# Local attention normalised behind the values' product, and new slots for softplus, copies, heads and tail, in a hybrid block kernel

## The chip, the cores and the metric

The kernel runs on one core of one Trainium2 chip. The metric is the device time in microseconds (us) of the whole kernel, 8 sequences (batches) in one launch. Engines are named as in the profile: PE (TensorE), DVE (VectorE), ACT (ScalarE), POOL (GpSimd) and SP (SyncE, which only issues DMAs here).

## The reference

For each of 8 sequences of 512 tokens of width 128, after a layer norm, the block adds four branches to its input, then a second layer norm and a small linear layer with a residual:

```python
xn = (x - mu) * rsqrt(var + 1e-05) * ln_g + ln_b
delta = softplus(dt_in @ w_dt + b_dt);  A = -exp(A_log)         # 128 channels, 64 states
h = exp(dt * A) * h + (dt * xt) * bt;   y = sum_n h * ct         # over 512 steps
scores = q @ k3 / sqrt(8) + bias       # 16 heads, 4 key heads, blocks of 32 queries, 96 keys
ao = softmax(mask(scores)) @ v3
conv = silu(conv4(x) + b_conv)
mem = x @ w_wm + b_wm + 0.3 * softmax(x @ dec.T / sqrt(128)) @ dec     # 512 memory rows
x1 = x + 0.2 * ao @ wo + 0.45 * (y + x * D) @ w_ssm_out + 0.15 * conv + 0.2 * mem
out = x1 + LN(x1) @ W2 + bias
```

## The kernel before

The state recurrence sets the frame. The 128 channels times 64 states are cut into 64 *units* (one unit: 2 channels by 64 states on 128 partitions, 512 steps along the free axis). Every engine has its own instruction stream, in which `body(B, p)` walks the 64 *slots* of batch B; the engines meet only at semaphores. In slot s:

- PE copies the input of unit s+2 to all state rows (`unit_u`, L911). In every fourth slot it sums a group of products over the states (`reduce_group`, L935).
- ACT takes the exponential of the decays of unit s+2 (`unit_exp`, L665). Both wait for the scan of unit s-2, whose buffers they fill again.
- DVE multiplies the unit's input by B (`unit_input`, L1189, three units of four) and runs the scan of unit s-1 (`unit_scan`, L1201).
- POOL multiplies two scanned units by C in odd slots (`pair_product`, L1389), and does the input product of each fourth unit (`pool_input`, L1405).

All else is hung into these slots by tables of numbers at the top of the file. `SCORES_AT` starts one of 16 attention blocks in slots 6, 9, ..., 51, and the `_LAG` numbers say how many slots later each of its steps stands: bias and maximum on DVE (2), exponentials on ACT (3 and 4), the reciprocal of the sums on DVE (6), the division of the probabilities on POOL (`prob_norm`, L1394, listed at 5), the transposes on PE (`prob_transposes`, L951, 9), their copy on ACT (9), the product with the values on PE (`values`, L959, 11), and its copy on ACT (`ao_copy`, L695, 11). All four blocks of transposes and the values' result share one PSUM bank, `ptP`, so that the transposes of block k wait for `ao_copy` of block k-1.

`JOB_AT` places the matrix jobs that share the bank `jobP` (families p: next batch's projections; m: memory attention and convolution; t: the tail of the batch before). `AT` places the remaining steps: while batch B is scanned, its slots hold the end of batch B-1 (`project`, `residual`, `root2`, `normalise2`, `ffn`, `output`) and the preparation of batch B+1 (layer norm, softplus, the three bf16 parts of u, and q, k, v, B, C). The softplus is exp(-|x|) on ACT (L613), 1+e and back (L615, L617, for the part lost in rounding), the logarithm (L622), four steps on POOL (L332), then the parts. `normalise2` (L553) waits on POOL's `root2`. `PRE` lists the jobs that `front` runs for batch 0 before its slots, and `tail` finishes batch 7 behind its last slot.

An instruction that waits holds all that is behind it on its engine.

Of the kernel before, what the change touches and what calls it, by code (L numbers as in the profile page):

```python
# [39 lines left out]
MEM = {n: i for i, n in enumerate(["es0", "pt0", "conv", "es1", "es2", "pt1", "es3", "pt2", "pt3"])}  # L40
# [5 lines left out]
JOB_AT = {13: ("t", "back"), 15: ("p", "xaT"), 17: ("p", "xnT"), 19: ("p", "dtpre"), 21: ("p", "v"),  # L46
# [3 lines left out]
EMPTY_LAG = 0  # L50
LAST_PROJECT = {60: (0, 1), 61: (2, 3), 62: (4, 5), 63: (6, 7)}
# [4 lines left out]
    "reduce": 3, "y_copy": 5, "project": 1, "proj_copy": 12, "residual": 14, "aggr2": 16, "root2": 17,  # L56
    "normalise2": 20, "ffn": 25, "output": 29,

    "ln_stats": 0, "ln_aggr": 2, "ln_root": 4, "ln_apply": 11, "scale_xn": 12, "softplus_exp": 20,
    "softplus_logs": 21, "lost": 22, "log1p": 23, "dt": 24, "u": 25, "high": 28, "r": 30,  # L60
    "mid": 33, "lo": 35,

    "tanh": 40, "gate": 42,
# [4 lines left out]
ROWS_AT = {"store": 15, "rows": 14}  # L68
VALUE_DMA_AT = {4: (0, 1, 2, 3, 4, 5), 5: (6, 7, 8), 6: (9, 10, 11)}
PART_DMA_AT = {16: 0, 18: 1, 20: 2}  # L70
# [6 lines left out]
BIAS_LAG, EXP_LAG, INV_LAG, NORM_LAG, PT_LAG, PT_COPY_LAG, PV_LAG, AO_COPY_LAG = 2, (3, 4), 6, 5, 9, 9, 11, 11  # L77
# [38 lines left out]
def hybrid_block_kernel(nc, x, ln_g, ln_b, w_xproj, w_dt, b_dt, A_log, D_ssm, w_ssm_out, wq, wk, wv,  # L116
# [3 lines left out]
    with ctx:  # L120
# [138 lines left out]
        p_exp, p_inv, p_norm = sem("p_exp"), sem("p_inv"), sem("p_norm")  # L259
# [92 lines left out]
        def _(sp):  # L352
# [23 lines left out]
            def store_rows(B, p):  # L376

                wait(sp, sp_step, B * N_SP + SP["u"])
                sp.dma_start(dt_rows[p], dtv[:, :]).then_inc(rows_out, 16)
                sp.dma_start(u_rows[p], uv[32 * POOL_Q:32 * POOL_Q + 32, :]).then_inc(urows_out, 16)  # L380
# [23 lines left out]
            def body(B, p):  # L404
                for m in range(UNIT_PAIRS):
# [13 lines left out]
                    if not last(B):  # L419
                        if m == ROWS_AT["rows"]:  # L420
                            store_rows(B + 1, 1 - p)
# [53 lines left out]
            def front(B, p):  # L475
                load_weights()
                bias_out()
                store_rows(B, p)
                spread_parts(sp, B, p, 0)
                widen(B, p, 0)  # L480
                bias_back()
# [988 lines left out]
```

## Time and profile before

| | |
|---|---|
| median of 3 runs | 1112.58 us (1109.39 to 1113.99) |
| the profiled execution | 1114.23 us, of it 1112.4 us span |
| busy DVE, POOL | 979.3 us (88%), 955.6 us (86%) |
| busy ACT, PE | 837.5 us (75%), 830.9 us (75%) |
| slot 0 of batches 0 to 6 on DVE (layer norm statistics) | 37.3, 176.6, 308.8, 439.4, 571.5, 704.5, 834.6 us |
| last scan, last instruction on DVE | ends near 1086 us, 1109.7 us |

The span has a front of 37 us, eight batches of 130 to 139 us, and a tail of 23 us. Busy shares are means over stages in which different waits end last; the views of one stage tell more than they do. In a view of one engine's instructions, a bracket shows how long the engine sat idle before the instruction and what released it. In a view of waits the columns are the total, the number and the longest.

### The profile page before, as it was taken

Reading aid. Unit: us, or ns where it says so; the run is one execution under the profiler, and the core shown is the slowest. Engines: PE = TensorE matmul, PEld = TensorE weight load, DVE = VectorE, ACT = ScalarE, POOL = GpSimd, SP = SyncE. Lnnn points to the kernel's source line nnn. Section 1 sums busy time; section 2 is a strip of 40 time slices with the busy share of each in tenths; the row PEclk is TensorE's granted clock in tenths of the full one; section 3 lists DMA queues with packets and bytes.
Section 4 is the critical chain, followed back from the end, with each engine's and each line's share of the span. In section 5 each row is a group of like instructions: output and inputs, shape, how many; then the busy total and the mean of one; then the engine's idle time right before and its main releaser. Section 6 shows DMA issues by size and latency. Waiting matters only on the chain. (4 is left out here: it accounts for less than half of the span.)

```text
span 1112.4 us, 19145 instructions
## 1 busy us (share of the span) xinstructions
PE 830.9 (75%) x4151; PEld 339.3 (30%) x4151; DVE 979.3 (88%) x2299; ACT 837.5 (75%) x2255; POOL 955.6 (86%) x675
## 2 busy tenths in 40 slices
PE   5367878688777786877778777867868778677775
PEld 2023333233323332333323333323332333232332
DVE  2688999979997999979999699897999799999991
ACT  4468886788778878687877887679887887858871
POOL 6369988989898988988899898899989898979892
PEclk9556998978997989979898798888899798989897
DMA  5845667647675666666676476665666566766630
GB/s 111 196 126 169 180 159 185 171 138 198 163 183 155 185 167 159 172 157 172 168 203 161 128 191 162 167 173 159 177 176 183 153 187 165 188 161 164 196 95 9
DMA packets 124391, 181.18 MB, mean 163 GB/s; under 512 B 29263, under 2 KB 41056, under 8 KB 124256
## 3 DMA queue, kind: packets, MB, share of 16 engines
q1 hardware_dynamic: 123968, 179.56, 61.4%
q14 instruction: 96, 0.79, 0.3%
q8 instruction: 39, 0.64, 0.3%
q10 hardware_dynamic: 288, 0.20, 0.1%
HBM read 170.79 MB, written 5.05 MB: 158 GB/s over the span
## 5 line engine op out<-in xcount | busy, mean ns | idle before, releaser
L1389 POOL TENSOR_TENSOR prod<-hst,C 128x1024 f32<-128x1024 f32 x256 | 602.0, 2354 | 94.9 <-DVE hst L1201 94.4
L1201 DVE TENSOR_TENSOR_SCAN hst<-decay,bank 128x512 f32<-128x512 f32 x384 | 459.5, 1209 | 3.0 <-DVE cv_a L1236 2.8
L1189 DVE TENSOR_TENSOR bank<-bank,B 128x512 f32<-128x512 f32 x384 | 263.1, 685 | 52.6 <-PE bank L911 34.8
L665 ACT ACTIVATE decay<-wide,A_rep 128x512 f32<-128x512 f32 x384 | 273.4, 715 | 41.5 <-DVE hst L1201 31.2
L911 PE MATMUL bank<-spread,sel_bc 96*128 96x512 bf16 x384 | 164.5, 434 | 101.0 <-DVE hst L1201 90.6
L679 ACT ACTIVATE prob<-s_sb,nmax 128x96 f32<-128x96 f32 x512 | 185.2, 365 | 0.9 <-DVE nmax L1214 0.5
L1405 POOL TENSOR_TENSOR uwide<-uwide,B 128x512 f32<-128x512 f32 x128 | 162.7, 1271 | 22.5 <-DMA uwide<-u_rows 22.5
L935 PE MATMUL bank<-prod,sel_red 128*32 128x512 f32 x1024 | 164.9, 722 | 0.0
L1201 DVE TENSOR_TENSOR_SCAN hst<-bank,uwide 128x512 f32<-128x512 f32 x128 | 155.4, 1214 | 2.7 <-POOL uwide L1405 2.7
L951 PE MATMUL bank<-ident,prob 128*96 128x128 f32 x512 | 85.9, 295 | 77.5 <-ACT ao L695 58.3
L944 PE MATMUL bank<-k,q 128*128 128x384 f32 x256 | 126.7, 580 | 22.3 <-DVE nmax L1214 22.2
L688 ACT ACTIVATE probT<-bank 96x512 f32<-96x512 f32 x128 | 74.9, 585 | 72.0 <-PE bank L951 71.6
L911 PEld LDWEIGHTS bank<-spread,sel_bc 96*128 96x128 bf16 x384 | 40.2, 106 | 228.0 <-DVE hst L1201 176.5
L665 ACT ACTIVATE bank<-wide,A_rep 128x512 f32<-128x512 f32 x128 | 87.2, 681 | 26.8 <-DVE hst L1201 26.6
L1394 POOL TENSOR_TENSOR prob<-prob,pinv 128x384 f32<-128x384 f32 x128 | 105.8, 826 | 0.0
L951 PEld LDWEIGHTS bank<-ident,prob 128*96 128x96 f32 x512 | 61.3, 137 | 135.4 <-issue 102.6
L1214 DVE CUSTOM_DVE_ANT_0 s_sb<-bank,bias 128x96 f32<-128x96 f32 x512 | 98.3, 250 | 0.0
L679 ACT ACTIVATION_READ_ACCUMULATOR prob<-s_sb,nmax 128x1 f32 x512 | 98.1, 192 | 0.0
L944 PEld LDWEIGHTS bank<-k,q 128*128 128x128 f32 x256 | 48.9, 216 | 87.0 <-DVE nmax L1214 48.6
L959 PE MATMUL bank<-probT,vw 96*8 96x128 f32 x1024 | 57.0, 298 | 14.7 <-ACT probT L688 9.8
L695 ACT ACTIVATE ao<-bank 128x128 f32<-128x128 f32 x128 | 34.1, 266 | 30.8 <-PE bank L959 30.5
L959 PEld LDWEIGHTS bank<-probT,vw 96*8 96x8 f32 x1024 | 19.9, 94 | 89.5 <-issue 57.1
(189 smaller groups left out, 1027.4 us busy)
## 6 DMA issues: line engine op xcount, KB each, us to landing
wide<-dt_rows SPq DMA_DIRECT2D x512, 256.0 KB, 4.7
uwide<-u_rows SPq DMA_DIRECT2D x128, 256.0 KB, 4.1
spread<-parts SPq DMA_DIRECT2D x66, 32.0 KB, 4.1
x_sb<-in_L_attn_x_dram SPq DMA_DIRECT2D x8, 256.0 KB, 4.5
dt_rows<-sp_t SPq DMA_DIRECT2D x8, 256.0 KB, 2.6
out_dram<-outb SPq DMA_DIRECT2D x8, 256.0 KB, 3.9
vw<-v_tok SPq DMA_DIRECT2D x80, 16.0 KB, 3.3
u_rows<-uv SPq DMA_DIRECT2D x8, 64.0 KB, 2.4
```

What stands on the lines that cost most here:

```text
L665: nc.scalar.activation(to, wide[m % SLOTS][:, s % 2, :], ACT.Exp, scale=A_rep[:, g:g + 1]).then_inc(exp_done, 1)
L679: ins = nc.scalar.activation(prob[:, k % 4, g, :], s_sb[:, k % 2, g, :], ACT.Exp, bias=nmax[:, k % 2, g:g + 1], scale=-1.0, accum_out=psum ...
L911: mm(uP[q][:, :], sel_bc[:, i, :, :].rearrange("k j n -> k (j n)"), spread[p][:, q, :], start=True, stop=True).then_inc(u_ready, 1)
L935: ins = mm(yP[32 * q:32 * q + 32, :], sel_red[:, i, :], prod[:, (i % 2) * 4 + q, :], start=(i == 0), stop=(i == GROUPS - 1), skip_group_ch ...
L944: mm(sP[:, 0:KVH * 3 * W], q4[:, k, :, :].rearrange("p r q -> p (r q)"), k4[:, :, k * W:k * W + 3 * W], start=True, stop=True).then_inc(s_ ...
L951: ins = nc.tensor.transpose(ptP[0:3 * W, g * 128:(g + 1) * 128], prob[:, k % 4, g, :], ident[:, :])
L1189: v.tensor_tensor(uP[s % 4][:, :], uP[s % 4][:, :], B2[p][:, :], ALU.mult).then_inc(dbx_done, 1)
L1201: v.tensor_tensor_scan(hst[:, s % 8, :], kept, into[:, :], 0.0, ALU.mult, ALU.add).then_inc(scan_done, 1)
L1214: ins = v.tensor_tensor_reduce(s_sb[:, k % 2, g, :], sP[:, g * 3 * W:(g + 1) * 3 * W], bias3[:, row, g, :], 1.0, BIG, ALU.add, ALU.min, nm ...
L1389: g.tensor_tensor(prod[:, 2 * (m % 4):2 * (m % 4) + 2, :], hst[:, 2 * (m % 4):2 * (m % 4) + 2, :], C2[p][:, :].unsqueeze(1).to_broadcast([ ...
L1394: g.tensor_tensor(prob[:, k % 4, :, :], prob[:, k % 4, :, :], pinv[:, k % 4, :].unsqueeze(2).to_broadcast([128, KVH, 3 * W]), ALU.mult) \
L1405: g.tensor_tensor(u, u, B2[p][:, :], ALU.mult).then_inc(gbx_done, 1)
```

## The change

1. **Attention.** The probabilities stay undivided. PE transposes them directly behind the exponentials (lag 6, was 9), multiplies by the values (lag 8, was 11), and in four further small products spreads the reciprocal sums over 32 rows each, into columns 128 to 255 of the same bank. ACT copies 256 columns of the bank (was 128; lag 9, now at the head of the slot behind `unit_exp`), and POOL multiplies the two halves (`output_norm`, 128 elements a partition; before, 384).
2. **Softplus and second norm.** The three ACT steps that stood in slot 20 stand in slots 24, 25 and 26; the logarithm moves from 21 to 28; `normalise2` from 20 to 23, `root2` from 17 to 19. The jobs B and C move from 34 and 35 to 24 and 25. POOL's four steps stand at 29 to 32 and not 22 to 25, the parts at 35 to 41. SP's stores and loads of these move with them.
3. **Heads.** `project` starts in slot 2 (was 1); the jobs `pt2`, `pt3` and `q` come one to two slots earlier.
4. **Front.** For batch 0 ACT goes from exp to the logarithm directly, DVE does 1+e and back in one instruction; dt is stored before u is there; two unit exponentials go ahead of the copies of q, and the copies of k go into slot 1.
5. **Tail.** Batch 7's projections start at slot 58 (was 60); terms 6 and 7 go ahead of the last reduction, 8 and 9 behind it; the bias of the last linear layer goes into the scores' bank, ahead of the second norm's transposes.

```diff
-MEM = {n: i for i, n in enumerate(["es0", "pt0", "conv", "es1", "es2", "pt1", "es3", "pt2", "pt3"])}
+MEM = {n: i for i, n in enumerate(["es0", "conv", "es1", "pt0", "es2", "pt1", "es3", "pt2", "pt3"])}
...
-          23: ("t", "zT"), 26: ("t", "ffn"), 30: ("m", "es0"), 34: ("p", "B"), 35: ("p", "C"), 37: ("m", "pt0"),
+          24: ("p", "B"), 25: ("p", "C"), 26: ("t", "zT"), 29: ("t", "ffn"), 33: ("m", "es0"),
...
-LAST_PROJECT = {60: (0, 1), 61: (2, 3), 62: (4, 5), 63: (6, 7)}
+LAST_PROJECT = {58: (0,), 59: (1,), 60: (2, 3), 61: (4, 5)}
...
-    "normalise2": 20, "ffn": 25, "output": 29,
+    "normalise2": 23, "ffn": 28, "output": 31,
...
-BIAS_LAG, EXP_LAG, INV_LAG, NORM_LAG, PT_LAG, PT_COPY_LAG, PV_LAG, AO_COPY_LAG = 2, (3, 4), 6, 5, 9, 9, 11, 11
+BIAS_LAG, EXP_LAG, INV_LAG, NORM_LAG, PT_LAG, PT_COPY_LAG, PV_LAG, AO_COPY_LAG = 2, (3, 4), 6, 9, 6, 6, 8, 9
...
-        prob = sb("prob", [128, 4, KVH, 3 * W])
+        prob = sb("prob", [128, 2, KVH, 3 * W])
...
+        ao_raw = sb("ao_raw", [128, 2, 2, 128])
...
                 nc.scalar.activation(sp_e[:, :], sp_e[:, :], ACT.Exp, scale=-1.0).then_inc(sp_step, 1)
+
+            def softplus_sum(B):
                 wait(act, sp_step, B * N_SP + SP["exp"])
                 nc.scalar.activation(sp_t[:, :], sp_e[:, :], ACT.Identity, bias=1.0).then_inc(sp_step, 1)
+
+            def softplus_less(B):
                 wait(act, sp_step, B * N_SP + SP["sum"])
                 nc.scalar.activation(sp_t[:, :], sp_t[:, :], ACT.Copy, bias=-1.0).then_inc(sp_step, 1)
 
             def softplus_logs(B):
 
-                wait(act, sp_step, B * N_SP + SP["less"])
+                wait(act, sp_step, B * N_SP + SP["exp" if first(B) else "less"])
...
-                    wait(act, pt_ready, B * NBLK + k - 3)
+                    wait(act, pt_ready, B * NBLK + k - 1)
...
                 wait(act, pv_ready, B * NBLK + k + 1)
-                if k == 0:
-                    wait(act, ready["t"], B * N_TAIL - N_TAIL + 1)
-                nc.scalar.activation(ao4[:, :, k * W:(k + 1) * W],
-                                     ptP[:, 0:128].rearrange("p (r q) -> p r q", r=REP), ACT.Copy).then_inc(ao_evac, 1)
+                wait(act, ao_norm, B * NBLK + k - 1)
+                nc.scalar.activation(ao_raw[:, k % 2, :, :].rearrange("p a c -> p (a c)"), ptP[:, 0:256],
+                                     ACT.Copy).then_inc(ao_evac, 1)
...
-                wait(pe, p_norm, B * NBLK + k + 1)
+                wait(pe, p_exp, B * NBLK + k + 1)
...
-                    ins = mm(ptP[32 * g:32 * g + HD, 0:128], vw[:, k, g, :], probT[:, g, :], start=True, stop=True)
+                    mm(ptP[32 * g:32 * g + HD, 0:128], vw[:, k, g, :], probT[:, g, :], start=True, stop=True)
+                wait(pe, p_inv, B * NBLK + k + 1)
+                for g in range(KVH):
+                    ins = mm(ptP[32 * g:32 * g + 32, 128:256], pinv[:, k % 4, g:g + 1].to_broadcast([128, 32]), ident[:, :],
+                             start=True, stop=True)
...
-                for n in range(8, N_PROJ - 1):
-                    project(B, p, n)
+                project(B, p, 6)
+                project(B, p, 7)
                 reduce_group(B, GROUPS - 1)
+                project(B, p, 8)
+                project(B, p, 9)
                 project(B, p, N_PROJ - 1)
                 tail_job("back", B, p)
+                wait(pe, s_max, NB * NBLK)
+                ffn_bias(sP)
                 tail_job("zT", B, p)
-                ffn_begin(B)
-                tail_job("ffn", B, p)
+                wait(pe, done["t"], job_count("t", B, "zT"))
+                ffn_half(0, sP)
+                filled(ffn_half(1, sP), "t", B, "ffn")
...
+                dve.wait_ge(sp_step, SP["exp"])
+                v.tensor_scalar(sp_t[:, :], sp_e[:, :], 1.0, 1.0, ALU.add, ALU.subtract).then_inc(sp_step, 2)
...
-            def prob_norm(B, k):
-                wait(pool, p_inv, B * NBLK + k + 1)
-                g.tensor_tensor(prob[:, k % 4, :, :], prob[:, k % 4, :, :],
-                                pinv[:, k % 4, :].unsqueeze(2).to_broadcast([128, KVH, 3 * W]), ALU.mult) \
-                    .then_inc(p_norm, 1)
+            def output_norm(B, k):
+
+                wait(pool, ao_evac, B * NBLK + k + 1)
+                if k == 0:
+                    wait(pool, ready["t"], B * N_TAIL - N_TAIL + 1)
+                g.tensor_tensor(ao4[:, :, k * W:(k + 1) * W], ao_raw[:, k % 2, 0, :].rearrange("p (r q) -> p r q", r=REP),
+                                ao_raw[:, k % 2, 1, :].rearrange("p (r q) -> p r q", r=REP), ALU.mult).then_inc(ao_norm, 1)
...
```

In the order of instructions, the first place is ACT in the body, from the second norm (`outb`) to the exponential behind the logarithm. `xn`, `sp_t` and `sp_l` are the softplus's tiles, `fT` the copy of job zT. Before:

```order
L553 ACTIVATE outb<-x,nbz,rz 128x128 x3
L695 ACTIVATE ao<-bank 128x4x32 [waits pv_ready]
L613 ACTIVATE xn<-xn 128x512 [waits sp_step]
...
L615 ACTIVATE sp_t<-xn 128x512 [waits sp_step]
...
L617 ACTIVATE sp_t<-sp_t 128x512 [waits sp_step]
...
L665 ACTIVATE bank<-wide,A_rep 128x512 [waits scan_done]
...
L688 ACTIVATE probT<-bank 96x512 [waits pv_ready,pt_ready]
...
L622 ACT_TABLE_LOAD
L622 ACTIVATE sp_l<-xn 128x512 [waits sp_step]
...
L665 ACT_TABLE_LOAD
```

and now:

```order
L560 ACTIVATE outb<-x,nbz,rz 128x128 x3
...
L705 ACTIVATE ao_raw<-bank 128x256 [waits ao_norm,pv_ready]
...
L599 ACTIVATE B_0<-bank 128x512 [waits p_job_ready]
L620 ACTIVATE xn<-xn 128x512 [waits sp_step]
...
L599 ACTIVATE C_0<-bank 128x512 [waits p_job_ready]
...
L624 ACTIVATE sp_t<-xn 128x512 [waits sp_step]
...
L748 ACTIVATE fT<-bank 128x512 [waits t_job_ready]
...
L628 ACTIVATE sp_t<-sp_t 128x512 [waits sp_step]
...
L633 ACT_TABLE_LOAD
L633 ACTIVATE sp_l<-xn 128x512 [waits sp_step]
...
L676 ACT_TABLE_LOAD
```

What stood within two slots now stands in six, with the copies of B, C and zT between.

The second place is PE within one attention block (`prob` the probabilities, `vw` the values, `pinv` the reciprocal sums, `sel_bc` the unit's input). Before:

```order
L951 MATMUL bank<-ident,prob 96x128 [waits ao_evac,p_norm]
L951 MATMUL bank<-ident,prob 96x128 x3
...
L911 MATMUL bank<-spread,sel_bc 128x512 [waits scan_done]
L959 MATMUL bank<-probT,vw 8x128 [waits pt_evac]
L959 MATMUL bank<-probT,vw 8x128 x3
```

and now:

```order
L967 MATMUL bank<-ident,prob 96x128 [waits ao_evac,p_exp]
L967 MATMUL bank<-ident,prob 96x128 x3
...
L927 MATMUL bank<-spread,sel_bc 128x512 [waits scan_done]
L975 MATMUL bank<-probT,vw 8x128 [waits pt_evac]
L975 MATMUL bank<-probT,vw 8x128 x3
L978 MATMUL bank<-ident,pinv 32x128 [waits p_inv]
L978 MATMUL bank<-ident,pinv 32x128 x3
```

The transposes no longer wait for POOL, and four products on `pinv` follow the values.

The third place is PE behind the last slot (`dec_m`, `wo_p`, `w_ssm`: terms of the projection). Before:

```order
L935 MATMUL bank<-prod,sel_red 32x512 x3
L1000 MATMUL bank<-ao,wo_p 128x512 [waits ao_evac] x4
L935 MATMUL bank<-prod,sel_red 32x512 [waits prod_done]
L935 MATMUL bank<-prod,sel_red 32x512 x3
L1003 MATMUL bank<-yT,w_ssm 128x512 [waits y_evac]
...
L820 MATMUL bank<-ident,outb 128x128 [waits l2_step,t_job_done]
L820 MATMUL bank<-ident,outb 128x128 x3
L1015 MATMUL bank<-bias_row,ones_row 128x512 [waits t_job_done]
L1008 MATMUL bank<-W,fT 128x128 x4
```

and now:

```order
L1020 MATMUL bank<-ao,wo_p 128x512 [waits ao_norm] x2
L951 MATMUL bank<-prod,sel_red 32x512 [waits prod_done]
L951 MATMUL bank<-prod,sel_red 32x512 x3
L1020 MATMUL bank<-ao,wo_p 128x512 [waits ao_norm] x2
L1023 MATMUL bank<-yT,w_ssm 128x512 [waits y_evac]
...
L1039 MATMUL bank<-bias_row,ones_row 128x512 [waits s_max]
L836 MATMUL bank<-ident,outb 128x128 [waits l2_step,t_job_done]
L836 MATMUL bank<-ident,outb 128x128 x3
L1028 MATMUL bank<-W,fT 128x128 [waits t_job_done]
L1028 MATMUL bank<-W,fT 128x128 x3
```

Two of the four `wo_p` terms stand behind the last reduction, and the bias product ahead of the second norm's transposes.

## Rows read from the trace of the kernel before

**Rows 1.** The page: busy time, share of the span and instructions of each engine.

```profile
PE 830.9 (75%) x4151; PEld 339.3 (30%) x4151; DVE 979.3 (88%) x2299; ACT 837.5 (75%) x2255; POOL 955.6 (86%) x675
```

**Rows 2.** The waits, longest first: who waited for whom, total us, times, longest.

```profile
PE bank L951 <- ACT ao L695: 58.3, 38, 3.9
...
DVE bank L1189 <- PE bank L911: 34.8, 24, 8.1
...
DVE pinv L1222 <- ACT prob L679: 25.3, 8, 3.8
...
DVE bank L1189 <- PE bank L944: 14.3, 14, 2.4
...
PE bank L990 <- ACT k L572: 7.6, 5, 1.7
```

**Rows 3.** DVE in order of time, batch 4, slots 23 to 33: the idle times.

```profile
619.24 0.70 DVE L1189 TENSOR_TENSOR bank<-bank,B 128x512 f32<-128x512 f32 x1 [2.31 <-PE bank L911]
...
624.77 0.18 DVE L1222 RECIPROCAL pinv<-psum_r 128x4 f32<-128x4 f32 x1 [3.71 <-ACT prob L679]
...
634.44 0.70 DVE L1189 TENSOR_TENSOR bank<-bank,B 128x512 f32<-128x512 f32 x1 [2.44 <-PE bank L944]
```

**Rows 4.** ACT in order of time, the same place of batch 4.

```profile
614.42 1.65 ACT L553 ACTIVATE outb<-x,nbz,rz 128x128 f32<-128x128 f32 x4 [0.62 <-POOL nbz L1411]
615.98 0.25 ACT L695 ACTIVATE ao<-bank 128x128 f32<-128x128 f32 x1
616.13 0.62 ACT L613 ACTIVATE xn<-xn 128x512 f32<-128x512 f32 x1
...
620.06 1.28 ACT L622 ACT_TABLE_LOAD   x1
621.36 0.63 ACT L622 ACTIVATE sp_l<-xn 128x512 f32<-128x512 f32 x1
622.00 1.28 ACT L665 ACT_TABLE_LOAD   x1
623.30 0.72 ACT L665 ACTIVATE decay<-wide,A_rep 128x512 f32<-128x512 f32 x1
```

**Rows 5.** PE in order of time, the same place of batch 4, and once behind it.

```profile
616.37 0.85 PE L951 MATMUL bank<-ident,prob 128*96 128x128 f32 x4 [3.38 <-ACT ao L695]
...
619.56 1.94 PE L935 MATMUL bank<-prod,sel_red 128*32 128x512 f32 x8
...
639.97 1.06 PE L935 MATMUL bank<-prod,sel_red 128*32 128x512 f32 x8
```

**Rows 6.** Busy us by stretch: that place in batch 4, and the same slots of batch 7.

```profile
616.00:640.00 24.00, 20.60 (x98) 9.67 (x99) 15.31 (x43) 20.43 (x57) 20.05 (x15) 0.72 0.44 129
1002.00:1020.00 18.00, 13.76 (x87) 5.73 (x79) 17.02 (x44) 13.67 (x44) 17.77 (x16) 0.90 0.71 181
```

The columns are: stretch, length, busy PE, PEld, DVE, ACT, POOL with instruction counts, granted clock, DMA share, GB/s.

**Rows 7.** The stretch of batch 7 for the scans (L1201) alone: busy DVE and count.

```profile
1002.00:1020.00 18.00, 10.91 (x10) 0.90 0.71 181
```

**Rows 8.** The page: groups of instructions, busy us, mean ns, idle before.

```profile
L1394 POOL TENSOR_TENSOR prob<-prob,pinv 128x384 f32<-128x384 f32 x128 | 105.8, 826 | 0.0
...
L959 PE MATMUL bank<-probT,vw 96*8 96x128 f32 x1024 | 57.0, 298 | 14.7 <-ACT probT L688 9.8
```

**Rows 9.** PE in order of time behind the last slots of batch 7.

```profile
1089.15 3.70 PE L1000 MATMUL bank<-ao,wo_p 128*128 128x512 f32 x8
1092.78 1.06 PE L935 MATMUL bank<-prod,sel_red 128*32 128x512 f32 x8
1094.57 1.13 PE L1003 MATMUL bank<-yT,w_ssm 128*128 128x512 f32 x2 [0.72 <-ACT yT L671]
...
1104.88 2.07 PE L1015 MATMUL bank<-bias_row,ones_row 1*128 1x512 f32 x2 [0.69 <-ACT fT L738]
```

**Rows 10.** POOL and PE in order of time: the last products, and the first inputs.

```profile
1082.02 6.97 POOL L1389 TENSOR_TENSOR prod<-hst,C 128x1024 f32<-128x1024 f32 x3
...
36.01 1.44 PE L911 MATMUL bank<-spread,sel_bc 96*128 96x512 bf16 x3 [9.44 <-DMA spread<-parts]
```

More of the change, by code:

```diff
@@ L648, in front @@
                             spread_parts(act, B, p, part)
+                        for s in range(AHEAD):
+                            unit_exp(B, s)
                         act.wait_ge(const_ready, 3)
                         act.wait_ge(head_tables, 3)
-                    if name == "k":
-                        for s in range(AHEAD):
-                            unit_exp(B, s)
-                    pre_job(name, B, p, front=True)
+                    if name != "k":
+                        pre_job(name, B, p, front=True)
             def unit_exp(B, s):
@@ L757, in body @@
                         unit_exp(B + 1, s + AHEAD - UNITS)
+                    k = block_at(s, AO_COPY_LAG)
+                    if k is not None:
+                        ao_copy(B, k)
                     if first(B):
+                        if s == 1:
+                            pre_job("k", B, p, front=True)
                         setup_step(s - SETUP_AT)
@@ L773, in body @@
                         probT_copy(B, k)
-                    k = block_at(s, AO_COPY_LAG)
-                    if k is not None:
-                        ao_copy(B, k)
                     t = memory_tile_at(s, M_EXP_LAG)
@@ L796, in body @@
                             softplus_exp(B + 1)
+                        if s == AT["sum"]:
+                            softplus_sum(B + 1)
+                        if s == AT["less"]:
+                            softplus_less(B + 1)
                         if s == AT["softplus_logs"]:
@@ L998, in project @@
                 elif n < 10:
-                    wait(pe, ao_evac, (B + 1) * NBLK)
+                    wait(pe, ao_norm, (B + 1) * NBLK)
                     ins = mm(jobP[:, :], wo_p[:, n - 6, :], ao4[:, n - 6, :], start=False, stop=False)
@@ L1004, in project, with ffn_half @@
                     filled(ins, "t", B, "proj")
-            def ffn_half(h):
+            def ffn_half(h, job=jobP):
                 for t in (2 * h, 2 * h + 1):
-                    ins = mm(jobP[:, t * D:(t + 1) * D], zT[:, t * 128:(t + 1) * 128], W2[:, :], start=False, stop=True,
+                    ins = mm(job[:, t * D:(t + 1) * D], zT[:, t * 128:(t + 1) * 128], W2[:, :], start=False, stop=True,
                              skip_group_check=True)
@@ L1014, in ffn_begin, with ffn_bias @@
                 fill("t", B, "ffn")
-                mm(jobP[:, :], ones_row[:, :], bias_row[:, :].unsqueeze(1).to_broadcast([1, NT, D]), start=True, stop=False,
+                ffn_bias(jobP)
+                ffn_half(0)
+            def ffn_bias(job):
+                mm(job[:, :], ones_row[:, :], bias_row[:, :].unsqueeze(1).to_broadcast([1, NT, D]), start=True, stop=False,
                    skip_group_check=True)
-                ffn_half(0)
             def tail_job(name, B, p):
@@ L1220, in inverse_sums @@
                 wait(dve, p_exp, B * NBLK + k + 1)
-                wait(dve, p_norm, B * NBLK + k - 3)
+                wait(dve, pv_ready, B * NBLK + k - 3)
                 v.reciprocal(pinv[:, k % 4, :], psum_r[:, k % 4, :]).then_inc(p_inv, 1)
@@ L1423, in body @@
                     if k is not None:
-                        prob_norm(B, k)
+                        output_norm(B, k)
                     if not first(B):
```

38 lines of the change are left out of this document (21 added, 17 removed), and 4 rows, old and new, of the table JOB_AT.

## The prediction, made before the changed kernel was run

> **What bounds the kernel now.** I read the page first. DVE is busy 979.3 us of 1112.4 and POOL 955.6 [rows 1], so DVE cannot end much before about 1037: its work plus some 58 us of front and tail (the first scan input comes at 36 us, the last scan ends 23 us before DVE's last instruction). The rest of DVE's idle time is 1112.4 - 979.3 - 58 = 75 us, and only that can be won in the batches. Then I read the waits: DVE waits for PE's unit inputs 34.8 us (8.1 of it once, in the front), for ACT's probabilities 25.3 us in 8 waits, for PE's scores 14.3 us [rows 2]. It hardly ever waits for POOL, so taking work from POOL is worth nothing by itself. Third, DVE in order of time. Each of batches 1 to 6 has the same hole in slots 23 to 31: 2.31 + 3.71 + 2.44 = 8.5 us in batch 4 [rows 3]. The others are 8.5, 6.9, 8.5, 6.1 and 6.9 us, together 45.5 or 7.6 a batch; batch 0 has 4.3, batch 7 has 1.0.
>
> Fourth, what the releasers did. ACT works without a pause through the second norm, three softplus steps, the logarithm and two table loads of 1.28 us [rows 4]. `ao_copy` stands behind the norm, PE's transposes wait 3.38 us for it, and the next unit input is queued behind them on PE [rows 5]; the exponentials of the scores stand behind the table loads, and DVE's reciprocal waits 3.71 us for them [rows 3]. The third gap is an echo: after PE's pause its granted clock in that stretch is 0.72, against 0.90 in batch 7 [rows 6], a mix of its two levels, 1.2 and 2.4 GHz; a reduction takes 1.94 us at the lower one where it takes 1.06 later [rows 5]. Batch 7 prepares no further batch, so it has no softplus, and there the hole is all but gone. That is the best evidence: the burst on ACT makes the hole.
>
> **Softplus, norm and copies (the largest term).** In batch 7 10 scans take 18.0 us [rows 7], so a slot is 1.8 us; ACT is busy 13.67 us of these [rows 6], so it has 24% or 0.43 us a slot to spare. Before, slots 19 to 23 hold on top: two 512-column steps of 0.6 us (job dtpre), the norm with its wait on POOL (0.62 + 1.6), three softplus steps (3 x 0.65), v (0.26), the logarithm with its loads (1.28 x 2 + 0.65 = 3.2), zT (0.6) [rows 4], together 9.4 us. Five slots spare 2.2, so ACT falls 7.2 us behind, and the first two gaps are 6.0: some 1.2 us are covered by the two slots that ACT and PE run ahead.
> After, the same sort of work stands in slots 21 to 28: 1.2 + 1.6 + 0.26 + 3 x 0.65 + 3.2 + zT 0.6, and now B and C too (2 x 0.6), 10.0 us; eight slots spare 3.4, so the backlog peaks at 6.6 us behind slot 28. The norm's wait on POOL (0.62) goes, since it stands 4 slots behind `root2` and not 3. With 1.2 us of cover that leaves 5.4 us; `output` at slot 31 gives ACT another 0.8 us of DVE time, so 4.6. The unevenness speaks for less: the scores' exponentials of slot 28 now stand ahead of the loads, the 3.7 us wait thus has no cause of its own, and with shorter pauses the echo (1.6 us on average) should not come. I take 4.0 us a batch in place of 7.6: -3.6 x 6 = -21.5 us, and -2 in batch 0 (half of its 4.3). Bounds: the hole as it is (0), and as in batch 7 (6 x 6.6 + 3.3 = -43).
> The trace has no drain in a table load: the logarithm starts 0.02 us behind a load that takes 1.28 [rows 4]. The Trainium skill ("ScalarE: Activation LUTs", What ACT_TABLE_LOAD costs) adds a drain of about 1.38 us to each switch, 2.66 us in all. By it the group in slot 28 would be 5.9 us long and not 3.2, and the sum would be 6 x 2.7 = 16 us higher; the row decides, and I leave it out.
>
> **Attention, POOL.** It loses 105.8 us of `prob_norm` [rows 8] and gets 128 products of a third of the size. By size that is 0.28 us each (826/3), bounded by 0.2 and 0.83: 36 us, bounds 25 and 106. So POOL falls by about 70 us, and by the waits above this buys nothing directly. The wait of the norm on `root2` gets shorter, which is in the term above. The new wait, POOL's `output_norm` on ACT's copy, holds `pair_product` and `pool_input` behind it. POOL starts slot s only when the scan of unit s is there, two slots behind ACT, so it costs nothing as long as ACT is less than 3.6 us late.
>
> **Attention, PE.** Four products of 128 columns a block are added, in four column groups, as `values` has. That row is busy 57.0 us in 128 blocks, 0.45 us a block for eight passes [rows 8]; mean 298 ns each shows that they overlap. I take 0.45, bounds 0.25 (a quarter of a reduction's 1.06, rows 5) and 2.4 (8 x 298 one behind the other). That is +57 us of PE work, 7 us a batch on 830.9; bounds 32 and 307. PE waits 58.3 us for `ao_copy` [rows 2] and more for scans, so this lies in pauses, except in slots 2 to 12, where `project` fills PE (see heads).
> The transposes wait no longer for DVE and POOL. They wait for `ao_copy` of the same slot, where before it was the slot before; ACT has it first behind `unit_exp`. That takes about 1 us of the lead of the unit inputs, and costs only where ACT is late already: +0, bounds 0 and +12 (1 us in each of 12 blocks).
>
> **Attention, ACT and DVE.** The copy has 256 columns for 128. From 0.25 us for 128 columns and 0.62 for 512 it will take 0.35 to 0.4 us [rows 4], 128 x 0.1 = 13 us more, of ACT's 275 idle. DVE's part does not change.
>
> **Heads.** PE waits 7.6 us in five waits for the copies of k before `project` [rows 2], and behind these DVE has gaps, 14 us over seven batches in slots 1 to 12. `project` one slot later takes that wait away, and the earlier `pt` and q jobs thin out ACT there. Against it stands the new PE work: 3 or 4 blocks in those slots, 1.6 us a batch. I take -2 us, bounds -12 and +12. The gaps at other places (some 0.8 us a batch around slot 52) get +2 us, since the jobs there move closer to the products.
>
> **Front.** Two ACT steps like the softplus step of 0.62 us in [rows 4], 0.65 with their gap, go from the chain exp, logarithm, parts, spread, first unit input [rows 10]; DVE's single instruction lies beside the table load. dt is stored one DVE step (0.7 us) earlier. -2 us, bounds -3 and +1 (u is stored later, and unit 3 needs it).
>
> **Tail.** POOL ends its last product at 1088.99, but PE reduces it only at 1092.78, since four `wo_p` terms stand ahead [rows 9, 10]. After, the reduction starts at 1089, ends at 1090.1, two terms (1.85) cover the copy of y, and the last term starts at 1091.95 and not 1094.57: -2.6. PE is free in time, for its earlier terms start two slots sooner. The bias product of 2.07 us stands on the chain [rows 9] and goes under the second norm: -2.1. Together -4.7, bounds -2 and -6.
>
> **Sum.** -21.5 - 2 + 0 - 2 + 2 - 2 - 4.7 = -30 us. From the profiled execution's 1114.2 that gives 1084; it lies 1.6 us above the median of the runs, so I forecast 1083 against 1112.6, or 2.7% faster.
>
> **Rivals.**
> *The hole closes* (0.24). If the lateness of ACT is covered by slots 24 to 28, only batch 7's 1.0 us remains: -43, heads -8, front and tail -6.7: 1055. For it: the three causes of rows 3 are each moved away from one another. Against it: 10.0 us of ACT work in eight slots do not fit into 3.4, and B and C now stand in the middle of it.
> *The hole moves* (0.12). It is as long as before in slots 24 to 33, since the logarithm with its loads is undivided and the transposes wait on the same slot's copy. Then the front, the tail and the heads remain, -8.7: 1104 against the median. For it speaks that backlogs of 7.2 and 6.6 us hardly differ.
> *PE becomes the bound* (0.06). Where PE's work in a slot passes 1.8 us, each added product delays the next unit input. In batch 7 it is busy 13.76 of 18.0 us at a clock of 0.90 [rows 6], so it has 0.42 us a slot, and a block's 0.45 us falls on three slots. At the clock of the hole it would not fit: 20.60 of 24.0 are taken [rows 6]. If the clock stays low, all 57 us come on the path, against gains of 30: 1140. It decides when PE has less than 0.15 us a slot left.
>
> What POOL does is no rival, for if its relief brought nothing at all the sum would be the same.
>
> **Numbers.** The forecast has 0.58 (its own range 1070 to 1095). The range for 8 in 10 goes from 1060, most of the way to the first rival and short of all bounds together, to 1104, the second. Half a per cent is 5.6 us, about what a measurement of this kernel can tell from no change: the second rival is half inside it. Faster 0.86, same 0.07, slower 0.07.
>
> **What would show it.** Batches 1 to 6 should take about 126 us each (now 130 to 133). DVE's gaps in slots 23 to 33 should sum to 3 to 5 us a batch, behind the logarithm at slot 28 to 31 and not before it; the wait of the reciprocal for the probabilities should fall from 25.3 to under 8 us. POOL's busy time should be near 885 us, PE's near 885, ACT's near 850. The new products should be busy about 57 us. On the end, the bias product should stand beside the second norm, and DVE's last instruction 18 us behind the last scan. The forecast is wrong if the waits for unit inputs stay above 30 us, or if new waits of DVE for PE are spread over all blocks.

## The result, and the profile after

| | after | before |
|---|---|---|
| median | 1187.53 us (1183.06 to 1189.20, 4 runs) | 1112.65 us |
| ratio, 95% interval | 1.0671 [1.0634, 1.0709] | |
| profiled execution, its span, its granted clock | 1187.11 us, 1185.3 us, 0.857 | 1114.23 us, 1112.4 us, 0.871 |

The changed kernel is 6.7% slower, where 2.7% faster was forecast: 104 us lie between the forecast and the measurement. The experiments below find them in two lines of the change, and with these two mended the kernel runs at 1083.2 us. Of all the runs reported here, one of experiment 8 (2344 us) and three of the kernel before in the last set were in a slower state and are left out of medians and ratios.

The page's busy times, which answer to [rows 1]:

```profile
PE 866.9 (73%) x5175; PEld 368.5 (31%) x5175; DVE 987.3 (83%) x2300; ACT 854.8 (72%) x2253; POOL 910.3 (77%) x675
```

No engine's work explains the loss: DVE has 8 us more, PE 36, POOL 45 less. The idle time of DVE grew by 65 us. The waits (total us, times, longest), which answer to [rows 2]:

```profile
PE bank L967 <- ACT ao_raw L705: 86.4, 68, 4.7
DVE x L1273 <- PE bank L836: 59.9, 8, 9.0
PE bank L975 <- DMA vw<-v_tok: 44.2, 7, 7.2
DVE bank L1219 <- PE bank L927: 38.7, 32, 8.0
DVE pinv L1252 <- ACT prob L690: 16.9, 8, 3.1
DVE bank L1219 <- PE bank L960: 14.6, 15, 3.1
```

Two rows are new in size. The transposes of the probabilities wait 86.4 us for ACT's copy (58.3 before), and PE waits 44.2 us for transfers of `vw`, the values, seven times: once in each of batches 1 to 7. DVE's wait for the residual (`x`, L1273) is its echo. Batch 1 in order of time, first SP's queue, then PE, then DVE:

```profile
197.49 3.89 SPq L462 DMA_DIRECT2D vw<-v_tok  x6
201.54 1.27 SPq L407 DMA_DIRECT2D wide<-dt_rows  x2
202.91 2.25 SPq L462 DMA_DIRECT2D vw<-v_tok  x3
205.29 1.50 SPq L407 DMA_DIRECT2D wide<-dt_rows  x2
206.89 1.93 SPq L462 DMA_DIRECT2D vw<-v_tok  x3
```

```profile
210.94 0.61 PE L975 MATMUL bank<-probT,vw 96*8 96x128 f32 x8 [6.38 <-DMA vw<-v_tok]
211.33 0.65 PE L978 MATMUL bank<-ident,pinv 128*32 128x128 f32 x8
211.91 0.61 PE L927 MATMUL bank<-spread,sel_bc 96*128 96x512 bf16 x1
212.45 1.94 PE L951 MATMUL bank<-prod,sel_red 128*32 128x512 f32 x8
214.32 1.65 PE L960 MATMUL bank<-k,q 128*128 128x384 f32 x2
```

```profile
217.59 0.69 DVE L1273 TENSOR_TENSOR x<-bank,x_sb 128x512 f32<-128x512 f32 x1 [8.17 <-PE bank L836]
...
243.09 0.18 DVE L1252 RECIPROCAL pinv<-psum_r 128x4 f32<-128x4 f32 x1 [3.14 <-ACT prob L690]
```

SP issues 12 transfers of values one after another, 0.64 to 0.75 us each, starting only when block 0 has its scores; the last issue ends at 208.8. The values' product of block 0 now stands in slot 14 instead of 17, so it waits 6.38 us, and the next input, the reduction and the scores stand behind it, at the lower clock as well (1.94 us where [rows 5] also has 1.06). DVE then idles 8.17 us. Its gaps at this place in batches 1 to 7 are 8.17, 6.37, 6.76, 6.80, 9.04, 6.33 and 8.44, together 51.9 us.

The hole that the prediction followed got shorter and now stands in slots 28 and 29, but it shrank less than forecast: its two large gaps are 3.14 + 1.49 us in batch 1 and together 3.9 to 5.5 in batches 2 to 6, and all gaps of slots 23 to 33 come to 5.4 us a batch, where 4.0 was taken. The tail and the products:

```profile
1172.10 0.69 DVE L1273 TENSOR_TENSOR x<-bank,x_sb 128x512 f32<-128x512 f32 x1 [7.94 <-PE bank L836]
...
1181.86 0.69 DVE L1291 TENSOR_TENSOR outb<-bank,x 128x512 f32<-128x512 f32 x1 [7.64 <-PE bank L1028]
```

```profile
L975 PE MATMUL bank<-probT,vw 96*8 96x128 f32 x1024 | 54.9, 289 | 49.1 <-DMA vw<-v_tok 44.2
L1427 POOL TENSOR_TENSOR ao<-ao_raw 128x128 f32<-128x128 f32 x128 | 58.4, 456 | 15.3 <-ACT ao_raw L705 15.1
```

From the start of the last scan to that of `outb` it is 18.9 us (23.75 before). The values' row [rows 8] kept its busy time, but its idle time rose from 14.7 to 49.1.

### The profile page after: what moved, and what is told of

Same layout as the page of the kernel before. It is cut to its first block and busy times, and to the rows that moved or that the text cites. A ratio compares the mean times of both kernels' runs of the same rounds, so it can differ in the third digit from the quotient of the medians.

```text
span 1185.3 us, 21303 instructions
## 1 busy us (share of the span) xinstructions
PE 866.9 (73%) x5175; PEld 368.5 (31%) x5175; DVE 987.3 (83%) x2300; ACT 854.8 (72%) x2253; POOL 910.3 (77%) x675
## 5 line engine op out<-in xcount | busy, mean ns | idle before, releaser
L1219 DVE TENSOR_TENSOR bank<-bank,B 128x512 f32<-128x512 f32 x384 | 263.0, 685 | 64.5 <-PE bank L927 38.7
L951 PE MATMUL bank<-prod,sel_red 128*32 128x512 f32 x1024 | 173.5, 757 | 0.3 <-POOL prod L1419 0.3
L967 PE MATMUL bank<-ident,prob 128*96 128x128 f32 x512 | 90.5, 307 | 86.4 <-ACT ao_raw L705 86.4
L960 PE MATMUL bank<-k,q 128*128 128x384 f32 x256 | 123.6, 567 | 6.6 <-DVE nmax L1244 6.2
L975 PE MATMUL bank<-probT,vw 96*8 96x128 f32 x1024 | 54.9, 289 | 49.1 <-DMA vw<-v_tok 44.2
L705 ACT ACTIVATE ao_raw<-bank 128x256 f32<-128x256 f32 x128 | 47.2, 369 | 35.0 <-PE bank L978 34.8
L1427 POOL TENSOR_TENSOR ao<-ao_raw 128x128 f32<-128x128 f32 x128 | 58.4, 456 | 15.3 <-ACT ao_raw L705 15.1
L960 PEld LDWEIGHTS bank<-k,q 128*128 128x128 f32 x256 | 46.2, 206 | 71.2 <-issue 52.5
L1001 PE MATMUL bank<-mdiag,mprob 128*128 128x128 f32 x256 | 45.0, 331 | 17.2 <-ACTq L717 9.2
```

The lines of the kernel that those rows point to most:

```text
L951: ins = mm(yP[32 * q:32 * q + 32, :], sel_red[:, i, :], prod[:, (i % 2) * 4 + q, :], start=(i == 0), stop=(i == GROUPS - 1), skip_group_ch ...
L960: mm(sP[:, 0:KVH * 3 * W], q4[:, k, :, :].rearrange("p r q -> p (r q)"), k4[:, :, k * W:k * W + 3 * W], start=True, stop=True).then_inc(s_ ...
L967: ins = nc.tensor.transpose(ptP[0:3 * W, g * 128:(g + 1) * 128], prob[:, k % 2, g, :], ident[:, :])
L1219: v.tensor_tensor(uP[s % 4][:, :], uP[s % 4][:, :], B2[p][:, :], ALU.mult).then_inc(dbx_done, 1)
```

## The experiments

A measurement gives the median, the ratio to the kernel before and its 95% interval. The kernel before ran on the same chip each time (1117.3, 1116.6, 1115.2, 1114.2 and 1116.7 us in the five sets); the ratio is estimated from all the runs, so it is not exactly the quotient of the medians. Where an edit of numbers says enough, only that is shown.

**1. The transfers of the values earlier.**

```diff
-VALUE_DMA_AT = {4: (0, 1, 2, 3, 4, 5), 5: (6, 7, 8), 6: (9, 10, 11)}
+VALUE_DMA_AT = {0: (0, 1, 2, 3, 4, 5), 1: (6, 7, 8), 2: (9, 10, 11)}
...
-                    wait(sp, s_ready, B * NBLK + 1)
+                if not first(B):
+                    wait(sp, pv_ready, B * NBLK)
```

> The changed kernel with one edit: the twelve DMAs that lay out the values of each batch are issued at SP's steps 0 to 2 (slots 0 to 5) and not 4 to 6, and wait for the last product with the values of the batch before and not for this batch's first scores. Theory A (the first product with the values, now in slot 14 and not 17, waits for these DMAs, and PE holds all behind it): PE's wait for vw (44 us) and DVE's wait for the residual (52 us in the batches) go, 1187 falls to about 1135. Rival B (PE's added products and the transposes' wait on the same slot's copy make the kernel slower, and the DMA wait only lies where PE would wait anyway): DVE waits elsewhere for nearly the same time, 1175 or more.

Measured: 1134.94 us, 1.0166 [1.0115, 1.0217], 52.6 us less. DVE's wait for the residual is 13.4 us instead of 59.9, and PE's for the transfers is gone, as theory A said. The first cause is shown. What is left to explain is 52 us between this kernel and the forecast.

**2. The transfers late, the lags later.** The changed kernel with three buffers of probabilities and these lags:

```diff
-... = 2, (3, 4), 6, 9, 6, 6, 8, 9
+... = 2, (3, 4), 6, 12, 9, 9, 11, 12
```

> The changed kernel with the attention steps at later slots: transposes and their copy at lag 9, values at 11, copy and product at 12 (three buffers of probabilities). The values' DMAs stay where they are. Theory A: the first product with the values stands in slot 17 again, the wait for its DMAs is nearly gone, about 1135 as with the early DMAs. Rival B: all of PE's and ACT's added work and the wait on the same slot's copy are still there, 1175 or more.

Measured: 1159.01 us, 1.0346 [1.0274, 1.0418]. PE's wait for the transfers is down to 4.3 us, so the slot of the values' product decides whether their transfers are late. But the kernel was 24 us slower than experiment 1, between the two theories, and the transposes waited 98.7 us for ACT's copy, which neither theory named.

**3 and 4. The change in two parts.** First the kernel before with the attention part and the early transfers, then the changed kernel without the attention part.

> The kernel before with the attention part of the change alone (undivided probabilities, four more products, wider copy, division on POOL, new lags), with the values' DMAs early; softplus, norm, jobs, heads, front and tail as before. Theory A: PE's added 57 us lie mostly in pauses, 1113 to 1130. Rival B: 1150 or more.

> The changed kernel with the attention part taken back: the division on POOL, lags and copies as before; softplus, norm, jobs, heads, front and tail at their new places. By the sum of the prediction without the attention terms it is 1083 to 1095: DVE's hole in slots 23 to 33 falls from 7.6 to about 4 us a batch, front -2, tail -4.7. Rival C (the new places of softplus and jobs are themselves no gain, the hole only moves): 1105 or more.

Measured: 1152.17 us, 1.031 [1.0256, 1.0364], and 1109.86 us, 0.9951 [0.9918, 0.9984]. The attention part costs some 35 us beside its transfers, as rival B had it; in its trace (of the fastest of its five runs, 1140.6 us) the transposes wait 117.2 us for the copy. The rest gains little, as rival C had it: DVE's idle time in slots 21 to 34 of batches 1 to 6 falls from 7.8 us a batch to 2.8, but that in slots 35 to 47 rises from 0.5 to 4.2, where the gate waits for ACT's tanh and the memory's reciprocal for its exponentials. The change had moved the tanh and the gate two slots forward (from 40 and 42 to 38 and 40).

**5. Without the four sum products** (experiment 1's kernel; what it leaves out is the division by the right sums).

> e1 (values early) without the four products that spread the reciprocal sums; ACT still copies 256 columns, of which half are then meaningless, so the output is not divided by the right sums. Theory D (PE's added 0.45 us a block is on the path): of the 25 us that e1 lies above the rest of the change alone (1110), nearly all go, 1110 to 1118. Theory E (the order: the transposes wait for the copy of the same slot, and its copy back for them): PE's products lie in pauses, 1128 to 1135.

Measured: 1152.14 us, 1.0331 [1.0274, 1.0388]: above both theories, 17 us *slower* without products that were busy 52.8 us in experiment 1. They are thus no cost. The granted clock fell from 0.883 to 0.861, and the work that is left got longer: PE as a whole is busy 843.2 us against 844.9 with the products, the transposes of the probabilities alone 94.1 against 87.6. That led to experiment 9.

**6. The transposes a slot later** (experiment 1 with lags 7, 7 for 6, 6).

> e1 with the transposes and their copy at lag 7 and not 6, so one slot behind the copy of the block before; products and copies are all there. Theory E: 1112 to 1122, and PE's wait for the copy (86 us) falls below 60. Theory D: 1130 to 1137.

Measured: 1135.77 us, 1.0161 [1.0091, 1.0231]. The wait moved and did not shrink: PE waited 21.5 us for the copy of the values, but 97.8 for the copy of the transposed probabilities, ahead of the values. The time lies in theory D's range, but D's reason, PE's added work, is excluded by experiment 5.

**7. The gate later, without the attention part.** Slot 42 is where the kernel before has its gate.

> The rest of the change alone (e4, 1110) with the convolution one slot later (39), its gate in slot 42 and not 40 (three slots behind and not two), and the memory jobs behind it where they stood before (43 to 59, q at 60). Theory F (the gain of the softplus's new slots is lost at the gate, 2.1 us a batch, and at the memory jobs around it, and can be had): about 1095. Theory G (the hole is only ACT's work, and shows wherever DVE next needs ACT): 1105 to 1112.

Measured: 1110.45 us, 0.9935 [0.9904, 0.9966]; as experiment 4, so theory G.

**8. Front and tail alone, on the kernel before.**

> The kernel before with the changes of front and tail alone. By the prediction -6.7 us: 0.994 of before, about 1106 if before is 1112.6. If the last terms of the projection come too late in their old slots, only the bias product's 2 us and the front's 2 us show.

Measured: 1115.8 us, 0.9978 [0.9933, 1.0023]. In its trace the first scan starts 0.5 us earlier and the end behind the last scan is 2.8 us shorter; the times can't tell that from nothing.

**9. The sum products on a constant** (experiment 1; also without the right sums).

```diff
-                wait(pe, p_inv, B * NBLK + k + 1)
-                    ins = mm(..., pinv[:, k % 4, g:g + 1].to_broadcast([128, 32]), ident[:, :],
+                    ins = mm(..., ident[:, 0:32], ident[:, :],
```

> The kernel of e1 with the four sum products of a block multiplied from the constant identity instead of the reciprocals, and without the wait for the reciprocal: the output is not divided by the right sums, but the matrix engine has the same 53 us of small products as e1 and e5 has not. Theory K (the clock: with less work between its waits the matrix engine is granted less, and its chain of transposes, values and inputs gets longer; e1 0.883 and 1134.9, e5 0.861 and 1152.1): the products' work brings the time back, 1130 to 1140 at a granted clock of 0.88. Theory W (it is the order that the wait for the reciprocal makes between the vector and the matrix engine that helps e1): no wait, so the time stays with e5 at 1148 to 1156, though the clock may rise.

Measured: 1136.18 us, 1.0183 [1.0122, 1.0244], granted clock 0.875 to 0.897 in its four runs, against 0.857 to 0.861 in those of experiment 5; this is theory K. The busy times of 900 us in the middle, first of experiment 5, then of this one (stretch, length, busy PE, PEld, DVE, ACT, POOL, granted clock):

```profile
200.00:1100.00 900.00, 678.97 (x3432) 277.75 (x3430) 801.28 (x1900) 698.07 (x1867) 740.88 (x534) 0.87 0.63 164
```

```profile
200.00:1100.00 900.00, 688.77 (x4418) 298.67 (x4416) 818.48 (x1923) 708.59 (x1902) 756.17 (x543) 0.91 0.63 165
```

Nearly 1000 more matrix instructions come to only 10 us more of busy time, and DVE gets 17 us more done (the trace is of the fastest of the four runs, 1126.4 us, so some of this is its own). It is the products' work that gives the time back, not the wait on the reciprocals. That it does so through the clock fits every number here, but no run holds the clock fixed, so this step is inferred.

**10. ACT's copy of the values in the values' own slot** (experiment 1 otherwise).

```diff
-PT_COPY_LAG, PV_LAG, AO_COPY_LAG = ..., 6, 8, 9
+PT_COPY_LAG, PV_LAG, AO_COPY_LAG = ..., 6, 8, 8
...
                         unit_exp(B + 1, s + AHEAD - UNITS)
-                    k = block_at(s, AO_COPY_LAG)
-                    if k is not None:
-                        ao_copy(B, k)
...
                         probT_copy(B, k)
+                    k = block_at(s, AO_COPY_LAG)
+                    if k is not None:
+                        ao_copy(B, k)
```

> The kernel of e1 with ScalarE's copy of the values in the slot of the values themselves and behind the copy of the transposed probabilities, as the kernel before has it, instead of at the head of the next slot. Theory P (the wait of the transposes for this copy, 85.9 us in 72 waits in e1 against 58.3 in the kernel before, comes from the copy's place, and is what the attention part costs beside the values' transfers): the wait falls to 60 or less and the time to 1110 to 1122. Theory Q (ScalarE's slots are full, the wait is of its load and not of the place): wait and time stay, 1130 to 1140, or ScalarE now waits for the values ahead of its softplus or norm and the time rises above 1140.

Measured: 1083.22 us, 0.9707 [0.9639, 0.9775], better than either theory had it. The waits of experiment 1 (first) and of this one, in each the transposes for the copy and DVE for its unit inputs:

```profile
PE bank L969 <- ACT ao_raw L707: 85.9, 72, 4.7
...
DVE bank L1221 <- PE bank L929: 39.2, 32, 8.4
```

```profile
PE bank L969 <- ACT ao_raw L707: 31.1, 28, 3.5
...
DVE bank L1221 <- PE bank L929: 18.0, 19, 8.1
```

**11 and 12. The transfers early without the attention part**, on experiment 7 and on the kernel before.

> The kernel of e7 (attention as in the kernel before, the rest as in the changed one, gate and convolution a slot or two later) with the values' transfers issued in slots 0 to 2 instead of 4 to 6. The kernel before has 14.7 us of waits ahead of the values' product. Theory V (part of that wait is on the path even with the values at slot 17): 3 to 10 us less than e7, 1100 to 1107. Theory N (it is hidden, since the vector engine is two slots ahead there): 1110 as e7.

> The kernel before with the values' transfers in slots 0 to 2 and nothing else. Theory V: 3 to 10 us less than the kernel before (a ratio of 0.991 to 0.997). Theory N: within 0.3% of it. It also says how much of e3's time is of its attention part and how much of the transfers' place.

The "slots 0 to 2" of these texts are SP's steps of two slots each, as in experiment 1.

Measured: 1112.17 us, 0.9963 [0.9936, 0.9991], and 1114.03 us, 0.9983 [0.9951, 1.0014]. This is theory N twice: with the values' product at slot 17 their transfers' place is worth nothing that can be measured. It costs time only together with the new lag.

**13 and 16. The copy's place alone, both ways.** The changed kernel with only this mended, its transfers still late; and the kernel before with only this made worse (its copy moved from the end of slot 11 of a block to the head of slot 12).

> The changed kernel with ScalarE's copy of the values in the values' own slot, behind the copy of the transposed probabilities, and the values' transfers left in slots 4 to 6. Theory S (the two costs add: transfers 52 us, the copy's place 52 us): 1130 to 1140, with the residual gaps behind the transfers still there. Theory H (ScalarE's queue now stands still behind the late values as well, so that the gaps by the transfers grow): 1150 to 1175. Theory M (the copy is hidden behind the transfers): 1180 or more.

> The kernel before with ScalarE's copy of the values moved from the end of slot 11 of a block to the head of slot 12, the one edit of the attention part that e10 takes back, and nothing else. Theory P (a copy at the head of the slot of the next block's transposes makes them, and every input behind them on the matrix engine, wait for the end of ScalarE's work of that slot): the wait ahead of the transposes rises from 58 us to 85 or more and the time to 1140 to 1170. Theory Q (the place costs only together with the changed attention): 1110 to 1122.

Measured: 1139.43 us, 1.0219 [1.017, 1.0267], so 48 us less (theory S); and 1161.03 us, 1.0412 [1.0367, 1.0456], so 47 us more (theory P). The wait of the transposes fell from 86.4 us in 68 waits in the one and rose from 58.3 us in 38 waits in the other, here experiment 13 and then 16:

```profile
PE bank L967 <- ACT ao_raw L705: 33.7, 30, 3.2
```

```profile
PE bank L951 <- ACT ao L695: 131.0, 74, 6.3
```

Batch 3 of experiment 16 shows the mechanism, PE first, then ACT:

```profile
495.00 0.41 PE L959 MATMUL bank<-probT,vw 96*8 96x128 f32 x8
...
503.21 1.06 PE L951 MATMUL bank<-ident,prob 128*96 128x128 f32 x4 [6.31 <-ACT ao L695]
```

```profile
498.80 1.65 ACT L553 ACTIVATE outb<-x,nbz,rz 128x128 f32<-128x128 f32 x4 [1.74 <-POOL nbz L1411]
...
500.35 0.61 ACT L613 ACTIVATE xn<-xn 128x512 f32<-128x512 f32 x1
501.00 0.63 ACT L615 ACTIVATE sp_t<-xn 128x512 f32<-128x512 f32 x1
501.66 0.63 ACT L617 ACTIVATE sp_t<-sp_t 128x512 f32<-128x512 f32 x1
502.20 0.67 ACT L665 ACTIVATE bank<-wide,A_rep 128x512 f32<-128x512 f32 x1
502.81 0.26 ACT L695 ACTIVATE ao<-bank 128x128 f32<-128x128 f32 x1
```

The values were ready at 495.4. In [rows 4] the copy stands directly behind the norm and ahead of the three softplus steps; at the head of the next slot it comes behind them and behind one more unit exponential, and the transposes, with all of PE behind them, wait for it.

**14. The attention part alone, mended in both places.**

> The kernel before with the attention part alone, the values' transfers in slots 0 to 2, and ScalarE's copy in the values' slot. e3 (the same with the copy at the head of the next slot) was 1152. Theory P (the copy's place is the cost of the attention part, and the undivided softmax by itself costs nothing or gains): 1095 to 1112, so at or below the kernel before. Theory R (the undivided softmax costs time by itself, and e10 is fast by the moved steps): 1120 or more.

Measured: 1118.42 us, 1.0013 [0.9981, 1.0046], between the two theories: the undivided softmax by itself neither gains nor loses anything that can be measured. So experiment 10's gain is not a sum of the parts: the rest is worth 7 us on the kernel before and 35 on this one.

**15, 17 and 18. Past experiment 10.** The gate two slots later (slot 42, as in the kernel before) with later memory jobs and projections; the convolution, its tanh and the gate one slot later and nothing else; and experiment 10 again.

> The kernel of e10 with the convolution at slot 39, its gate at 42 and the memory jobs and the last projections as in e7. e10 still has 1.5 to 3.6 us of idle time a batch of the vector engine in slots 35 to 47, most of it ahead of the gate. Theory G (a gap that closes if ScalarE is given two slots more): 1073 to 1080. Theory T (the gap goes to wherever the vector engine next needs ScalarE, as between e4 and e7): 1080 to 1087.

> The kernel of e10 with the convolution, its tanh and its gate one slot later (39, 39, 41), and nothing of e15's other edits. Theory L (e15 lost its 14 us by the last projections, q and the memory jobs, whose work now lies closer ahead of the next batch's first slots: idle of slots 1 to 12 rose from 9 to 23 us over batches 1 to 7): this one keeps e10's time or gains up to 5 us, 1078 to 1084. Theory T (the gate's later place lengthens other waits): 1088 to 1097.

> The kernel of e10 once more: 1080 to 1090, a ratio of 0.966 to 0.976, if its time holds.

Measured: 1096.83 us, 0.9834 [0.98, 0.9868]; 1090.11 us, 0.977 [0.972, 0.982]; 1084.05 us, 0.9719 [0.9671, 0.9767]. Experiment 10 holds and is the best version found, 2.8% under the kernel before; both later gates lose. Experiment 15 lies above both of its theories, and experiment 17 is theory T, other waits get longer: the transposes wait 49.4 us for the copy (50.5 in experiment 15, 35.5 in experiment 18), and 18.7 of it stand ahead of block 10, in slot 42, where experiment 18 has 1.7.

## Why the prediction was wrong

Two costs, each of about 50 us, and they add up:

| copy of the values on ACT | transfers late | transfers early |
|---|---|---|
| head of next slot | 1187.5 | 1134.9 |
| values' slot | 1139.4 | 1083.2 |

**Attention, PE: a step mis-sized.** "They wait for `ao_copy` of the same slot, where before it was the slot before [...] and costs only where ACT is late already: +0, bounds 0 and +12 (1 us in each of 12 blocks)". It is 47 to 52 us (experiments 16, 13 and 10). The mechanism was named, its size was not: I looked for a late ACT only in the hole of slots 23 to 33. Between experiments 1 and 10 the wait of the transposes fell from 85.9 us in 72 waits to 31.1 in 28, that is 44 waits and 54.8 us, or 1.2 us a wait. Behind it DVE's idle time fell from 30.9 to 13.5 us in slots 21 to 34, but from 34.9 to 3.7 in slots 48 to 64, summed over the batches. The waits ahead of blocks 8, 9, 10 and 15 (transposes in slots 36, 39, 42 and 57) went from 27.7 us to 0.4; they lie outside the hole, and the two kernels differ in the copy's place alone. [Rows 2] had shown 38 such waits, 58.3 us, already. The new products did fit into pauses, but longer waits of this kind were not free: 72.7 us more of them cost 47 us in experiment 16.

**The values' transfers: a step that is missing.** The lag of the values went from 11 to 8, with no term for what feeds them. In the kernel before, 4.7 of the 14.7 us of idle time of [rows 8] are waits for just these transfers, which I had not looked up:

```profile
PE bank L959 <- DMA vw<-v_tok: 4.7, 4, 2.0
```

So at lag 11 the product stood close behind its data, and three slots earlier it stood ahead of them. That is 52.6 us (experiment 1), or 56.2 in the table's other row.

**Softplus, norm and copies (-21.5 and -2): right in direction, with the parts mis-sized.** In the changed kernel the gain is mostly hidden. In experiment 10, DVE's idle time in slots 21 to 34 of batches 1 to 6 is 2.0 us a batch (7.8 before, 4.0 forecast), and in slots 35 to 47 it is 2.8 (0.5 before): -3.5 net a batch, -21 in all. In experiment 18, the same kernel again, the two are 2.5 and 1.5, or -26 in all. The sum is thus close to the forecast through a deeper cut and a new gap that has no term in it. Most of that gap is DVE's wait for the tanh ahead of the gate (12.2 us in 7 waits in experiment 10, 6.0 in experiment 18), and the change had moved both two slots forward. The norm's wait on POOL went as said, from 15.7 us in 8 waits to 4.9 in one. Experiment 4 shows the rival "the hole moves" at work where the attention part is absent. The reciprocal's wait for the probabilities is 16.9 us in the changed kernel and 0.5 in experiment 10; I had said under 8.

**Attention, the work.** PE's products were put at 57 us and measured at 54.6 (53.2 in experiment 10). That they lie in pauses was right by experiment 5, and they even gain time by experiments 5 and 9. PE as a whole was busy 867 us and not 885. The rival "PE becomes the bound" is refuted by experiment 5. POOL's product was put at 0.28 us by size and took 0.456 (the bounds were 0.2 and 0.83), so POOL is busy 910 us and not 885; this costs nothing, since no engine is seen to wait for this product. ACT came out at 855 us (850 forecast).

**Heads and slots near 60 (-2, +2).** DVE's gaps in slots 1 to 12 of batches 1 to 7 fell from 14.0 us to 8.8 (9.2 in experiment 10), more than was taken and inside the bounds. In slots 59 to 64 there were none before; they are 2.6 to 4.2 us a batch in the changed kernel, and in experiment 10 they are gone but for 1.4 us in batch 7, so they too hung on the copy.

**Front and tail (-2, -4.7).** The first scan starts 0.85 us earlier, and from the last scan to `outb` it is 4.85 us less. So the tail gave what was forecast and the front less than half of it.

**The sum.** The sign that I had set for being wrong, waits for unit inputs above 30 us, came true with 38.7. -30 us was forecast; with both places mended it is -29.4 us against the 1112.65 of the first table, -32.0 against the kernel before in its own set. That the two numbers meet at 1083 is partly luck, since the gains of the parts are not additive (experiment 14).

What stays open: why the moved steps are worth 7 us without the undivided softmax and 35 with it. Experiment 10 has less idle time of DVE in slots 21 to 47 (4.8 us a batch, 7.0 in experiment 4) and a higher granted clock (0.91 against 0.87), but what causes which was not taken apart.

## What to carry to other kernels

When a consumer moves forward, list every producer of each of its operands, its transfers included, and give each its own term; when a step moves past a slot's boundary in an in-order queue, count what now stands ahead of it in every repetition, not only where that engine is known to be late. A wait that the trace already shows ahead of such a step is a warning that a later release will be paid for, even where the engine as a whole idles a quarter of the time. Undoing one line of a large change at a time, on both kernels, told more than any reading of the two traces.

## What the hardware showed that I had not expected

Less work on TensorE made the kernel slower (experiments 5 and 9). Without the sum products the granted clock was 0.857 to 0.861 and the time 1152.1 us; with products that depend on nothing it was 0.875 to 0.897 and 1136.2 us. A reduction of eight passes takes 1.06 us at the upper of the two levels (2.4 GHz) and 1.94 at the lower (1.2 GHz), so where PE's waits are on the path, independent work put into its pauses can pay for itself, here with 16 us. Among the kernels with the same products the faster ones had the higher clock (0.857 at 1187 us, 0.883 at 1135, 0.91 at 1083). That may be effect as well as cause, since shorter waits make shorter pauses; and it does not hold across kernels with different work: the one before had 0.871 at 1114.

GpSimd's product of 128 elements a partition took 456 ns and that of 384 took 826 ns [rows 8], far from proportional. The 12 transfers of values, of 12 to 16 KB, took SP 0.64 to 0.75 us each to issue, 8 us for the set, beside 3.4 us (median, experiment 10) from one issue to its landing.
